# Entropy model ordered by side: two steps of one side together, a first tanh over 2048 columns, and the second gate folded into the last layer

## The reference, cut to what matters

```python
x = x + attention(_gn(x), ...)        # 1x1 projections q, k, v with prelu; softmax over 4096 positions
x = x + entropy(_gn(x), ...)
# entropy: for each of 192 channels, two sides of the same value
def _logits_cumulative(logits, ms, bs, fs):          # hidden widths 1 -> 3 -> 3 -> 3 -> 1
    for i in range(4):
        logits = einsum('cij,cjn->cin', softplus(ms[i]), logits) + bs[i]
        if i < 3:
            logits = logits + tanh(fs[i]) * tanh(logits)      # the gate of layer i
    return logits
lower = _logits_cumulative(xr - 0.5, ...)
upper = _logits_cumulative(xr + 0.5, ...)
sign = -sign(lower + upper)
likelihood = max(abs(sigmoid(sign * upper) - sigmoid(sign * lower)), 1e-6)
```

## Time and profile before

| | us |
|---|---|
| median of 3 runs | 4760.89 (4754.21 to 4761.35) |
| profiled execution, its time | 4754.35 |
| its span | 4752.5 |
| TensorE busy (matmul) | 4428.2 |
| VectorE busy | 4099.3 |
| ScalarE busy | 3736.5 |
| POOL busy | 813.8 |

### The profile page before, as it was taken

The page is one execution under the profiler, slowest core; times in us unless marked ns, Lnnn a source line. Parts: engine busy times, 40 slices in busy tenths (PEclk is TensorE's granted clock), DMA queues, the critical chain, the costliest instruction groups (busy, mean ns, idle before and its releaser), DMA issues.

```text
span 4752.5 us, 108300 instructions
## 1 busy us (share of the span) xinstructions
PE 4428.2 (93%) x38780; PEld 2977.4 (63%) x38780; DVE 4099.3 (86%) x5433; ACT 3736.5 (79%) x4214; POOL 813.8 (17%) x937
## 2 busy tenths in 40 slices
PE   5999989999899999999899998999989999899976
PEld 3888338873488735887258862688617885278821
DVE  6997899978999789996999969999698987999866
ACT  2777788868888698886988869787797877978787
POOL 4100201202022110211111120121201212022112
PEclk9999999999999999999999999999999999999998
DMA  2000321114211142111411124110331112311133
GB/s 68 25 21 25 97 73 53 38 39 100 68 51 36 44 103 62 46 44 40 111 51 53 36 58 104 40 61 28 78 89 49 47 41 75 93 49 34 40 93 94
DMA packets 155019, 280.19 MB, mean 59 GB/s; under 512 B 37441, under 2 KB 37921, under 8 KB 152706
## 3 DMA queue, kind: packets, MB, share of 16 engines
q1 hardware_dynamic: 154434, 272.69, 21.4%
HBM read 205.24 MB, written 50.33 MB: 54 GB/s over the span
## 4 chain that ended last, share of the span: by engine, by line
PE 72%; ACT 11%; DVE 7%; issue 7%; DMA 0%; ACTq 0%; POOL 0%; DVEq 0%; POOLq 0%
PE ps L1514 14%; PE ps L1512 14%; PE ps L1516 13%; PE ps L1288 9%; PE ps L1465 8%; ACT th L799 5%; ACT arena L792 4%; PE ps L1387 3%; PE ps L1321 3%; DVE th L1123 3%; PE ps L1373 3%; PE ps L1345 2%; DVE mxp L1191 2%; PE ps L1296 1%; PE ps L1280 1%
## 5 line engine op out<-in xcount | busy, mean ns | idle before, releaser
L1514 PE MATMUL ps<-v_sb,arena 128*128 128x192 f16 x8192 | 2026.8, 247 | 0.0
L1512 PE MATMUL ps<-v_sb,arena 128*128 128x193 f16 x8192 | 2017.9, 246 | 0.0
L1516 PE MATMUL ps<-v_sb,arena 128*128 128x193 f16 x8192 | 2009.9, 245 | 0.0
L755 ACT ACTIVATE arena<-ps 128x1024 f16<-128x1024 f32 x1024 | 1049.0, 1024 | 644.5 <-PE ps L1288 640.7
L1083 DVE TENSOR_TENSOR arena<-ps,arena 128x1024 f16<-128x1024 f32 x1024 | 1245.6, 1217 | 166.8 <-ACT ps L756 158.5
L1191 DVE TENSOR_REDUCE mxp<-ps 128x1 f32<-128x512 f32 x1792 | 1191.0, 688 | 41.3 <-PE ps L1465 29.3
L1123 DVE SCALAR_TENSOR_TENSOR th<-th,gates,ps 128x1024 f32<-128x1024 f32 x768 | 950.3, 1277 | 147.2 <-ACT th L799 140.1
L756 ACT ACTIVATE ps<-ps 128x1024 f32<-128x1024 f32 x1024 | 1044.4, 1020 | 0.0
L1514 PEld LDWEIGHTS ps<-v_sb,arena 128*128 128x128 f16 x8192 | 795.1, 97 | 262.7 <-issue 0.6
L799 ACT ACTIVATE th<-ps,biases 128x1024 f32<-128x1024 f32 x768 | 825.6, 1120 | 118.5 <-PE ps L1373 80.8
L1512 PEld LDWEIGHTS ps<-v_sb,arena 128*128 128x128 f16 x8192 | 792.1, 97 | 126.3 <-issue 10.8
(11 more groups left out here) (147 smaller groups left out, 3449.8 us busy)
## 6 DMA issues: line engine op xcount, KB each, us to landing
x<-x2d SPq DMA_DIRECT2D x1152, 64.0 KB, 2.3
arena<-x2d SPq DMA_DIRECT2D x768, 64.0 KB, 2.5
xp<-x_dram SPq DMA_DIRECT2D x18, 1536.0 KB, 10.1
shared<-x_dram SPq DMA_DIRECT2D x64, 384.0 KB, 3.9
x2d<-shared SPq DMA_DIRECT2D x64, 384.0 KB, 3.0
res<-x2d SPq DMA_DIRECT2D x96, 256.0 KB
out_dram<-res SPq DMA_DIRECT2D x96, 256.0 KB
kst<-shared SPq DMA_DIRECT2D x32, 256.0 KB, 3.2
```

The costliest lines, as they stand in the source:

```text
L755: act.activation(e_hi[:, q % 4, :].rearrange("p (k n) -> p k n", k=2), sc, ACT.Exp)
L1512: pe.matmul(acc, eh, v_sb[:, m, 0:C + 1], start=(m == 0 and t % 2 == 0), stop=False, skip_group_check=True)
L1514: pe.matmul(acc[:, 0:C], eh, v_sb[:, m, VW:VW + C], start=False, stop=False, skip_group_check=True)
L1516: ins = pe.matmul(acc, el, v_sb[:, m, 0:C + 1], start=False, stop=(m == MT - 1), skip_group_check=True)
```

## The change: what it does

- A slot pair `w` is now one side `d = w % 2` of a whole unit `w // 2` (all positions). `first_tanh(w)` is one ScalarE instruction over 2048 columns, two pairs ahead. Its input tile holds a whole unit; two such tiles replace three half ones.
- Per pair the order is: first layer of both slots, third layer of the pair before, second layer of both slots. Side work (values, maxima) stands at two places in the pair.
- The second gate is gone from VectorE (`FOLD = (True, True)`). The third layer runs per pair, as w3h on gated `th1` plus w3f on the plain tanh `th2`, accumulated in one bank: with h2 + g*tanh = W2*th1 + bias + g*tanh, the product w3*W2 and w3*g are prepared once by POOL.
- `th1` has 4 buffers and `th2` 2 (2 and 5 before). Both input halves of units 0 and 1 are loaded before the first tanh may start, and the rows for `t0` of pair 0 are loaded behind the store of the last block.

```diff
-X4R, T0R, HR1, HR2, XR, LUR = 3, 3, 2, 5, 4, 6
-LEAD = 4
+X4R, T0R, HR1, HR2, XR, LUR = 2, 3, 4, 2, 4, 6
+FOLD = (True, True)
-FIRST_AT = VB - V_LEAD + 1
+FIRST_AT = (VB - V_LEAD + 1) // 2
@@ tile_uses
-    for s in range(SLOTS + 2):
-        if s < SLOTS:
-            uses.append(("h1", s))
-        if 1 <= s <= SLOTS:
-            uses.append(("h2", s - 1))
-        if s >= 5 and (s - 1) % 4 == 0:
-            uses.append(("h3", (s - 1) // 4 - 1))
+    for w in range(HALVES + 1):
+        if w < HALVES:
+            uses += [("h1", 2 * w), ("h1", 2 * w + 1)]
+        if w >= 1:
+            uses.append(("h3", w - 1))
+        if w < HALVES:
+            uses += [("h2", 2 * w), ("h2", 2 * w + 1)]
@@ SyncE, phase_a
-                    load_side(l, row, 0)
                     store_x2(l, row, BLOCKS - 1)
                     for s in range(2):
                         sp.wait_ge(x2_stored[s], l * 64 + 64)
-                    load_x4(row, 1)
+                    load_side(row, 0)
+                    for u in range(X4R):
+                        load_half(row, 2 * u + 1)
@@ ScalarE, phase_a
+                def first_tanh(w, half=None):
+                    u, d = w // 2, w % 2
+                    if d == 0 and half != 1:
+                        loaded = 2 * SIDES + u // X4R * SIDES
+                        act.wait_ge(x4_in[u % X4R], l * X4_DMAS * 16 + loaded * 16)
+                    if w >= T0R:
+                        act.wait_ge(h1_mm, l * SLOTS + 2 * (w - T0R) + 2)
+                    if half is None:
+                        act.activation(t0[:, w % T0R, :, :], x4[:, u % X4R, :].rearrange("p (d n) -> p d n", d=2),
+                                       ACT.Tanh, bias=biases[:, d, 0, u:u + 1], scale=scl[:, u:u + 1]
+                                       ).then_inc(t0_ready, 2)
+                        return
...
+                for w in range(HALVES + (0 if proj else 3)):
+                    if w < HALVES:
+                        for c in (2 * w, 2 * w + 1):
...
+                            tanh("h1", c, th1[:, c % HR1, :, :], 1, h1_mm, t1_ready)
+                    if w + 2 < HALVES:
+                        first_tanh(w + 2)
+                    if proj and w == HALVES - 1:
+                        exps(pj(BLOCKS * PAIRS, 0), 0)
+                    if w < HALVES:
+                        for c in (2 * w, 2 * w + 1):
...
+                            tanh("h2", c, th2[:, c % HR2, :, :], 2, h2_mm, t2_ready)
+                    if proj and w == HALVES - 1:
+                        exps(pj(BLOCKS * PAIRS, 0), 1)
+                    for i in range(2):
+                        v = V_LEAD + 2 * w + i
+                        if proj and v < VB:
+                            negative(QK + v)
@@ VectorE, phase_a
+                for w in range(HALVES + (0 if proj else 3)):
+                    m = 2 * (w - FIRST_AT)
+                    if proj and 0 <= m < MAXES:
+                        first_reduce(m)
+                    if proj and m == MAXES:
+                        split_max(pj(BLOCKS, 0), pj(BLOCKS * MAXES, 0))
+                    if w < HALVES:
+                        for c in (2 * w, 2 * w + 1):
+                            gate("h1", c, th1[:, c % HR1, :, :], F1O, t1_ready, h1_ready)
+                    if 1 <= w <= HALVES:
+                        logits(l, w - 1, not proj)
+                    if proj and 0 <= m < MAXES:
+                        first_reduce(m + 1)
+                    if proj and m == MAXES:
+                        rows_out(pj(BLOCKS, 0), 0, l is None)
...
+                    for i in range(2):
+                        v = V_LEAD + 2 * w + i
+                        if proj and v < VB:
+                            value(QK + v)
@@ TensorE, third_layer
+                fold = folded(2 * w)
+                if fold:
                     for g in range(4):
-                        ins = pe.matmul(ps[32 * g:32 * g + 32, at + d, :], w3[:, u, :],
-                                        th2[:, (4 * u + g // 2 * 2 + d) % HR2, g % 2, :], start=True, stop=True)
+                        pe.matmul(ps[32 * g:32 * g + 32, at, :], w3h[:, u, :],
+                                  th1[:, (2 * w + g // 2) % HR1, g % 2, :], start=True, stop=False)
+                weights = w3f if fold else w3
+                for g in range(4):
+                    ins = pe.matmul(ps[32 * g:32 * g + 32, at, :], weights[:, u, :],
+                                    th2[:, (2 * w + g // 2) % HR2, g % 2, :], start=not fold, stop=True)
@@ TensorE, phase_a
+                def side_work(w, i):
+
+                    v, m = V_LEAD + 2 * w + i, 2 * (w - FIRST_AT) + i
+                    if proj and v < VB:
+                        value_bank(v)
+                    if proj and 0 <= m < MAXES:
+                        first_max(m)
+                    if proj and m == MAXES + 1:
+                        turn_max(pj(BLOCKS, 0), 0)
+
+                for w in range(HALVES + (0 if proj else 1)):
+                    if w < HALVES:
+                        first_layer(2 * w)
+                        side_work(w, 0)
+                        first_layer(2 * w + 1)
+                    if w >= 1:
+                        third_layer(l, w - 1)
+                    if w < HALVES:
+                        if proj and w == HALVES - 1:
+                            pe.wait_ge(max_in, pj(BLOCKS * 16, 16))
+                            scores(0, 0)
+                        second_layer(2 * w)
+                        side_work(w, 1)
+                        second_layer(2 * w + 1)
```

More of the change, by code:

```diff
@@ L125, in max_tiles, with folded, unfolded_before @@
     return list(range(min(PER_STEP * p, MAXES), min(PER_STEP * (p + 1), MAXES)))
+def folded(c):
+    return FOLD[c // 2 % 2]
+def unfolded_before(c):
+    return sum(not folded(i) for i in range(c))
 def tail_unit(i, last):
@@ L247, in program @@
         place = [0]
-        second = th2.rearrange("p s d n -> p (s d n)")
+        first = th1.rearrange("p s d n -> p (s d n)")
         def setup_area(*shape):
@@ L254, in setup_area @@
             place[0] += words
-            assert place[0] <= HR2 * 2 * N
-            area = second[:, place[0] - words:place[0]]
+            assert place[0] <= HR1 * 2 * N
+            area = first[:, place[0] - words:place[0]]
             return area if len(shape) == 1 else area.rearrange("p (a b) -> p a b", a=shape[0])
@@ L653, in phase_a @@
                         values(v)
[L654 to L657, removed]
+                for w in range(HALVES + 3):
+                    for i in range(2):
+                        v = V_LEAD + 2 * w + i
+                        if proj and v < VB:
+                            values(v)
+                    u = (w - 3) // 2
                     if 0 <= u < now:
-                        if (s - 5) % 4 == 0:
+                        if (w - 3) % 2 == 0:
                             sums(l, u, True)
-                        if (s - 5) % 4 == 1:
+                        else:
                             difference(l, u, True)
@@ L818, in phase_a @@
                 act.wait_ge(gn2_step, l * GN2_STEPS + 16)
-                for i in range(LEAD):
-                    first_tanh(i)
+                for half in range(2):
+                    first_tanh(0, half)
                     if proj:
-                        negative(3 + i)
+                        negative(3 + half)
+                first_tanh(1)
                 if proj:
-                    for n in range(3 + LEAD, QK + V_LEAD):
+                    for n in range(5, QK + V_LEAD):
                         negative(n)
[L826 to L842, removed]
@@ L1068, in logits @@
                     dve.wait_ge(v_done, l * VB + (VB + VB))
[L1069 to L1072, removed]
+                dve.tensor_scalar(logits_of(u, last)[:, d, :], ps[:, tile("h3", w), :], biases[:, d, 3, u:u + 1], None,
+                                  ALU.add).then_inc(lu_ready, 1)
             def result(l, i, last):
@@ L1163, in phase_a @@
                 now = 0 if proj else UNITS
[L1164 to L1186, removed]
@@ new lines, in first_reduce @@
+                def first_reduce(m):
+                    dve.wait_ge(max_mm, pj(BLOCKS * MAXES, m + 1))
+                    dve.tensor_reduce(mxp[:, m // BLOCKS, m % BLOCKS:m % BLOCKS + 1], ps[:, m % 2, :], AX_X,
+                                      ALU.max).then_inc(max_red, 1)
+                for w in range(HALVES + (0 if proj else 3)):
[14 more added lines that the diff above has]
+                    if w < HALVES:
+                        for c in (2 * w, 2 * w + 1):
+                            if not folded(c):
+                                gate("h2", c, th2[:, c % HR2, :, :], F2O, t2_ready, h2_ready)
+                    for i in range(2):
+                        v = V_LEAD + 2 * w + i
+                        if proj and v < VB:
+                            value(QK + v)
```

(4 more changed lines are left out.)

171 lines of the change are left out of this document (88 added, 83 removed).

## The result

The changed kernel takes 4819.3 us (median of 4 runs, 4815.92 to 4820.41) against 4759.5 us: a ratio of 1.0126, with a 95% interval of 1.0109 to 1.0144. It is slower by 1.3%. I had forecast 4742, and my range ended at 4812.

What follows compares the result with a forecast made beforehand. Three engines were taken to bound three stretches: TensorE beside values, VectorE beside maxima, ScalarE in the last image. Seven images at +0.5 and the last at -19 gave -15.5 on 4754.35: 4739, stated as 4742, range 4680 to 4812.

Steps and rivals of the forecast that it cites:

- At the head: a small loss: Start of an image: first tanh needs both halves of unit 0, loaded behind two side loads; +1 us, last image +1.6.
- Beside the values: Value stage: TensorE stalls 1.45 us for a value behind both second tanhs, pair 10.17 us; +12.5 us an image.
- rival C: Slower: stalls beside the values lower TensorE's granted clock, 1.7 us in each of six pairs; +71, about 4812; chance 0.10.
- Beside the maxima: Maxima stage: VectorE relieved, TensorE the new bound, 6.3 us a pair against half of 13.53; -6.5 us an image.
- rival A: Slower: beside the maxima TensorE's stream breaks at every group, a pair above 6.77 us; +67, about 4809; chance 0.18.
- To the attention: From last maximum to second attention pair: 21.1 us after against 27.6 before, a gain of 6.5 us an image.
- The last image: Last image, no side work: ScalarE binds, a unit takes 14.0 us against 15.36; -19 us in sum.
- Rival B: Faster: no stall beside the values, 8.8 us less an image; -61, about 4682; chance 0.16.
- Rival D: Slower: TensorE bounds everything and all added third layers count, 96 x 1.93 = 185 us; 4940; chance 0.03.
- The sum: Whole kernel: seven projecting images at +0.5 each, +3.5, last image -19; total -15.5, giving 4739, stated as 4742.

Runs made afterwards that it cites:

- e2: Changed kernel, first tanh's first half waiting only for unit 0's first half, whose second half loads ahead of the side rows: 4780.4 us, ratio 1.0048.
- e1: Changed kernel with the negative and value of a pair's first value bank moved behind the pair's first tanh and logits: 4743.1 us, ratio 0.9967.
- e6: Kernel before the change with each third layer issued twice, the second time over the first, all gates kept: 4914.3 us, ratio 1.0331.
- e3: Changed kernel with both the early value (e1) and the early head (e2): 4699.3 us, ratio 0.9878 to the kernel before.
- e8: Kernel of e3 with the first tanh as two instructions of 1024 columns again: 4709.6 us against 4699.3.

## Why the prediction was wrong, point by point

The direction was wrong. The failed step is "At the head: a small loss": priced at +1 us an image, it measured +6.0, because the late input came later than summed and because what an idle TensorE loses in its clock was put at nothing. That is 35 of the 80 us between 4739 and 4819. After it come the sizes of the two stages behind it, +2.6 and +2.8 us an image, whose mechanisms were right except for the clock.

- **The head.** I priced it at +1 us; it measured +6.0, 35 us over seven images. Two things failed. The late input: I took 0.45 us an issue for the larger side loads too, and the two together took 2.19 us (482.63 to 484.82) and not 0.9. The sum set the first tanh 1.2 us late; it is 2.5 us later relative to the turn than before (488.15, with the turn at 476.24), and 3.65 us later than e2 shows that this order allows. And I had not asked what the delay would do to TensorE, which idled 2.83 us and then ran the 24 matmuls at a mean clock of 0.65, +2.1 us. Over the seven images these 24 took 5.9 to 7.5 us, and 4.47 in every one before. In the last image the head cost 3.7 us and not 1.6. There my own sum would have said more: it puts the first tanh 9.2 us behind the store's issue, and before it came 6.4 us behind (4537.62 to 4544.03).
- **Beside the values.** The stall, its place and its cause were right: foreseen 1.45 us in a pair of 10.17, measured 1.55 in 10.40. The total is 15.1 and not 12.5: 0.23 in a pair, 0.46 in the first of them (its stall is 1.75 us), and in some images one fall of the clock. That size can be read: the stage takes 60.6 us in three of the seven images and 62.2 in four, with the same work; in one pair of the longer ones shown above first layer and third layer take 1.73 and 1.94 us and not 1.09 and 1.07. So rival C was part of the truth: 1.6 us once in this stage in four images, and not 1.7 in every pair, and once more beside the maxima in the same four; and at every head, where I had not placed it.
- **Beside the maxima.** TensorE streams, as forecast, so rival A falls (it wanted a pair above 6.77). A pair takes 6.42 and not 6.31: the step into the third layer is 1.02 us and not the 0.97 I took, and so is the one before the second maximum. Where the clock stays the stage takes 100.4 us, 1.6 more than the 98.8 foreseen, and the clock after the wait for the first maximum takes 1.6 more in four images: -3.7 and not -6.5.
- **To the attention.** -5.7 against -6.5. The order of the steps was right.
- **The last image.** A unit takes 13.97 us (14.0 foreseen), and the two pairs without first tanhs 12.7 from first tanh to third layer (12.5). Up to the first tanh of slot 44 the gain was 6.8 us and not 12.6: the head took 2.1 of the difference, and the rest are waits in the first units, which I had put at nothing. The largest is for the side rows:

```profile
4661.87 2.73 PE L1430 MATMUL ps<-arena,w1s 64*64 64x512 f32 x16 [2.44 <-DMA arena<-x2d]
```

From slot 44 to the end the gain was 7.2 us and not 6.6, so -14.0 in all.
- **Rival B** (no stall) had no ground in the kernel as written; as an edit it is e1. **Rival D** (all added third layers count): e6 shows that the added work alone would have cost 157 us in the old order, close to its 185; in the new order the removed gates pay for it. My argument against D, that VectorE ends the waits beside the maxima, did not hold as put: added third layers cost nearly their full length there although another engine is busier. By the Trainium skill, Perfetto Trace Analysis, Identifying the Most-Contended Engine, the engine with the highest occupancy comes first; but for TensorE that section does not take the matmul busy share as the measure, and looks at its useful matmul work and its weight loads. The prediction left that out. The weight loads were busy 63% and VectorE 86%, so read in full the rule points at VectorE by these two shares, not at rival D. VectorE then lost 434 us of work and the time rose, while e1 and e2 changed no engine's work by design and gave 76 and 39 us: here no share of busy time told what would pay.
- **The sum.** 7 x (6.0 - 1.0) = 35, 7 x 2.6 = 18, 7 x 2.8 = 20, 7 x 0.8 = 6, and 5 in the last image: 84 us. Less 0.8 ahead of the first turn and 0.1 us of attention an image it is 82, against 81 between the -15.5 forecast and the +65.8 measured on the profiled executions.

## What to carry to other kernels

When steps are grouped, ask for each small side task whose result an in-order queue waits for whether it now stands behind the group: here one negative and its value behind two tanhs cost 76 us with its aftermath, and moving them was enough to turn a loss of 1.3% into a gain of 0.3%. When a gate or any elementwise step is folded into matmuls, decide by stage: it paid beside the maxima (13.6 us an image with what follows), where it shortens the round through the PSUM tiles, and lost 2.2 us beside the values, where TensorE was already the bound. A delay at a stage's head can cost its own length and then what TensorE's clock loses beside the idle: 3.65 and 2.1 us here.

## What the runs showed of the hardware

- TensorE's clock fell to the lower of its two levels (1.2 of 2.4 GHz) at each of the seven heads of the kernel after: in six of them with an idle of 2.83 us, in one with idles of 1.03 and 1.48 us. The 24 matmuls behind took 5.9 to 7.5 us and not 4.47. Idles of 0.9 to 2.0 us at the same place in e2 and e3 left the clock alone, in all fourteen images.
- Beside the values it fell behind 4 of 35 stalls of 1.55 or 1.75 us, where matmul groups of 1.09 and 1.07 us took 1.73 and 1.94. Why one of equal stalls and not the next stays open.
- A load of 128 KB took SyncE 0.56 us to issue (median) and one of 64 KB 0.37, so a byte was cheaper to issue in the larger load. At the head two side loads of 128 KB took 2.19 us. Input loads of 128 KB landed 4.8 us after the issue (median), those of 64 KB after 2.4.
- A tanh over 2048 columns took 2.09 us, where two of 1024 in e8 took 2.36: 0.3 us for one instruction less.
